# TensorE's order in a round of the two graph convolutions: eight sums together, the other work behind them

## The reference

```
xn  = layernorm(x)
# conv: twice, with its own weights
msg = relu(x[src]);  agg = segment_sum(msg, dst)
h   = relu((x + agg) @ w1 + b1) @ w2 + b2
# beside it a linear attention over all nodes
k, v = layernorm of (xn @ wk.T), (xn @ wv.T) per head;  kv = k.T @ v / S
x = x + relu(2 * conv(relu(conv(xn)))) + (xn @ wq.T) @ kv @ wo.T + bo
x = x + layernorm(x) @ weight.T + bias
```

## Time and profile before

| | us |
|---|---|
| median of 3 runs | 5125.66 |
| lowest and highest | 5112.02, 5127.13 |
| profiled execution | 5140.41 |
| its span in the trace | 5138.7 |
| first and last addition of the two convolutions | 225.1, 2500.5 |

### The profile page before, as it was taken

How to read it: one execution, slowest core, us unless ns; L and a number is a source line. 1 busy time by engine, 2 the same in 40 slices (tenths; PEclk the granted TensorE clock), 3 DMA queues, 4 the chain that set the end, 5 groups by cost and what they waited for, 6 DMA issues and landing times. The chain is left out here.

```text
span 5138.7 us, 69292 instructions
## 1 busy us (share of the span) xinstructions
PE 3250.9 (63%) x14347; PEld 2386.3 (46%) x14348; DVE 2963.7 (58%) x7108; ACT 1986.1 (39%) x4909; POOL 2901.0 (56%) x2929
## 2 busy tenths in 40 slices
PE   4477777777566677676677426666666532099980
PEld 1255555555455555555567414444444432066650
DVE  5677777777556666666556755555555584022223
ACT  0444444444333344343332135555555443033331
POOL 0377777777577777777204247777777735500006
PEclk6588888888778888888889758888888855599995
DMA  2434343433233333333212101111111342511115
GB/s 82 141 111 115 114 115 112 115 110 110 81 102 99 101 103 102 100 103 101 69 38 53 26 16 27 27 27 27 27 27 27 25 134 76 193 53 55 55 55 145
DMA packets 265996, 410.73 MB, mean 80 GB/s; under 512 B 77510, under 2 KB 182883, under 8 KB 265508
## 3 DMA queue, kind: packets, MB, share of 16 engines
q0 software_dynamic: 120320, 275.83, 21.3%
q1 hardware_dynamic: 145444, 132.39, 8.1%
HBM read 324.85 MB, written 83.11 MB: 79 GB/s over the span
## 5 line engine op out<-in xcount | busy, mean ns | idle before, releaser
L1463 PE MATMUL conv_ps<-conv_msg,conv_S 128*128 128x256 f32 x3328 | 1104.0, 481 | 596.7 <-DVE ACC L1473 265.7
L1463 PEld LDWEIGHTS conv_ps<-conv_msg,conv_S 128*128 128x128 f32 x3328 | 746.8, 238 | 836.4 <-issue 465.1
L1439 POOL DMA_INDIRECT conv_msg<-conv_table,GI x832 | 882.8, 1061 | 307.6 <-issue 259.2
L1439 POOL DMA_INDIRECT conv_msg<-relu_xn_table,GI x832 | 807.1, 970 | 358.4 <-issue 248.1
L1473 DVE TENSOR_TENSOR ACC<-ACC,conv_ps 128x256 f32 x1664 | 701.8, 422 | 515.2 <-issue 260.6
L2377 POOL DMA_INDIRECT gat_msg<-attn_table,GI x832 | 829.4, 997 | 266.6 <-issue 253.3
L2430 PE MATMUL gat_ps<-gat_M,gat_S 128*128 128x260 f32 x1664 | 596.1, 506 | 383.7 <-DVE ACC L2484 233.7
L1448 ACT ACTIVATE conv_S<-iota_row,LOC 128x128 f32<-128x128 f32 x1664 | 507.2, 387 | 387.8 <-PE conv_ps L1463 378.5
L2430 PEld LDWEIGHTS gat_ps<-gat_M,gat_S 128*128 128x128 f32 x1664 | 374.9, 245 | 528.2 <-issue 473.1
L3033 POOL DMA_INDIRECT combine_y<-expert_out,combine_at x98 | 94.5, 964 | 579.8 <-ACTq L3021 560.3
L2484 DVE TENSOR_TENSOR ACC<-ACC,gat_ps 128x260 f32 x832 | 350.2, 421 | 57.6 <-PE gat_ps L2430 23.1
(11 more groups left out here) (535 smaller groups left out, 5466.7 us busy)
## 6 DMA issues: line engine op xcount, KB each, us to landing
expert_in<-heads_zrow SPq DMA_DIRECT2D x53, 256.0 KB, 3.0
experts_xe<-expert_in SPq DMA_DIRECT2D x106, 128.0 KB
expert_out<-experts_y SPq DMA_DIRECT2D x106, 128.0 KB, 1.7
conv_msg<-relu_xn_table,GI POOLq DMA_INDIRECT x832, 2.8
conv_msg<-conv_table,GI POOLq DMA_INDIRECT x832, 2.8
gat_msg<-attn_table,GI POOLq DMA_INDIRECT x832
relu_xn_table<-begin_rx SPq DMA_DIRECT2D x49, 128.0 KB, 1.7
xnT<-begin_xt SPq DMA_DIRECT2D x49, 128.0 KB, 1.8
```

The source lines that it names most:

```text
L1439: pool.indirect_dma_start(self.msg[:, h * RING + k, :], None, table, bass.IndirectOffsetOnAxis(ap=self.m.GI[:, t:t + 1], axis=0)).then_inc ...
L1463: self.nc.tensor.matmul(self.ps[k % self.NB][:, 0:D], self.S[:, r % 2, k, :], self.msg[:, r % self.DEEP * RING + k, :], start=True, stop=T ...
```

## The change

In both convolution stages TensorE issues the eight sums of a round one after the other, and then the other work of the round. Before, four sums came, then the other work, and then four sums. The small matmuls at the end of an odd round stay last.

```
@@ stage_conv1, block.tensor
                 if r < ROUNDS:
                     rounds.pe_ready(pe, r)
-                    rounds.pe_sums(pe, r, 0, RING // 2)
+                    rounds.pe_sums(pe, r, 0, RING)
                 if here(i := turn_of(r, 4)):
                     kv.pe_sums(pe, i)
...
                 if here(u := turn_of(r, NodeNet.START + 1)):
                     net.pe_first(pe, u)
-                if r < ROUNDS:
-                    rounds.pe_sums(pe, r, RING // 2, RING)
                 if here(g := turn_of(r, 1, GROUPS)):
```

## The result

The changed kernel takes 5282.46 us (median of 4 runs, 5280.60 to 5286.83) against 5126.40 beside it: 1.0312 times the time before, with a 95% interval of 1.0292 to 1.0332. The forecast was slower, 5208 us, with a range of 5125 to 5305. Direction and range hold; the size was off by a factor of nearly two: +82 forecast, +156 measured.

The account below looks back on a forecast made before the run. VectorE's loop with ScalarE was taken to bound the first convolution, GpSimd's gathers the second. Over 48 pairs, 29 us and 53 us made 82 us on 5125.66, giving 5208 us, range 5125 to 5305.

Parts of the forecast that it names:

- What bounds each stage: First convolution: VectorE's pace, new waits paid in full; second: GpSimd's gathers, with 2.3 us a pair of slack for VectorE.
- Nothing is gained in the middle of the round: Side work between the sums was hidden behind VectorE's work; removing it gives at best GpSimd's 9.6 us in 400 us.
- rival C: Both convolutions: sums end earlier and GpSimd's waits for sums in the first go, 5100 us; chance 0.07.
- Second convolution, even round: Addition 3 to the odd round's addition 0 takes 6.5 us, 1.1 us above the slack: 53 us in all.
- First convolution, even round: Addition 3 to next sum 0 takes 5.7 to 7.4 us against VectorE's 6.14 us of work: 0.4 us a pair.
- another wait, which I have not priced, stands ahead of the first addition: Listed sign that the forecast is wrong: an unpriced wait ahead of a round's first addition; no size given.
- the likeliest case alone: Whole kernel: the narrower span of 5165 to 5260 us, inside the full range.
- First convolution, odd rounds: ScalarE's ReLU behind late side work delays finished rows only when one pair in eight starts low: 0.2 us a pair.
- The clock decides: Moved side work was expected to start at the lower clock in most pairs, losing 1.7 us or more.
- Rival A: Both convolutions: side work runs at the full clock and nothing changes, 5126 us; chance 0.14.
- Rival B: Both convolutions: low clock lasts through most even and part of odd side work, 216 us more, 5340 us; chance 0.15.
- The rule on keeping TensorE busy: TensorE in both convolutions: read naively, sums and side work run together at full clock, so the extra would be 0.

Follow-up runs that it names:

- root_first: The changed kernel, with ScalarE's square root put ahead of its copy of turned rows in the first convolution: 5218.26 us, 1.0190 times the kernel before.
- filler: The changed kernel, with matmuls nobody reads added on TensorE ahead of its waits for sums 4 and 6 of even rounds: 5146.65 us, 1.0056 times before.

## Why the prediction was right in direction and short in size

- **What bounds each stage**: right, as far as the runs show. The first convolution paid each new wait of VectorE in full; the second lost only what went beyond its slack, and there the gathers stopped being the bound.
- **Nothing is gained in the middle of the round**: right; no run showed a gain from it, and rival C (faster) is out.
- **Second convolution, even round**: 6.5 us from addition 3 to addition 0 and 53 us in all were forecast; the pair shown has 7.04 us, the mean of the 44 pairs is 7.0, and the stage grew by 66 to 81. The low clock covered the side work more fully than the 3.4 us that the earlier trace rows suggested, since it had fallen ahead of sum 4 and lasted from there to the end of the side work.
- **First convolution, even round**: the step that failed. The forecast compared sum 0 with VectorE's need and got 0.4 us a pair. It took VectorE's 6.14 us of own work as cover, and didn't ask what that work itself waits for. Its first instruction L444 needs ScalarE's root, which is queued behind the copy that needs the moved transposes. That wait is 1.9 us a pair where there were 0.3. root_first, which frees the root alone, gives 76 of the stage's 88 us back: some 54 at the end of even rounds, and 22 at the end of odd ones, whose side work then ran at the full clock in all pairs. The 12 that remain stand at the end of even rounds and are the forecast's own term (0.4 x 48 = 19). The prediction had named the case among its signs of being wrong ("another wait, which I have not priced, stands ahead of the first addition"), but gave it no price. Its range was wide enough to take it in; the likeliest case alone (5165 to 5260) was not. That the range holds is in part luck.
- **First convolution, odd rounds**: the ReLU's chain was named, and priced at 0.2 us a pair, 10 us, for one pair in eight with a low start. In the changed kernel 21 of 45 pairs had a low stretch in that side work and waited 2.09 us in place of 1.06: 0.5 us a pair, 22 us.
- **The clock decides**: right, and now shown. With the even rounds' side work at the full clock the changed order costs 29 us instead of 160 (filler), and 26 of these are the waits behind odd side work, nearly all in pairs where that still ran low. Rival A, whose rows were at the full clock, had the right price for that clock, but not the clock. Rival B had the size closer (216 us), but for the second stage 120 and for ScalarE's root nothing.
- **The rule on keeping TensorE busy** (the Trainium skill, TensorE: Matmul & The Clock Gate, "Why this matters for your kernels"): by it, idle gaps between bursts cost clock. The trace agrees: the clock fell within the 3.87 us idle, and was 0.50 from there through nearly all of the side work. It is the idea that eight sums in a row in the program are a burst on the engine that doesn't hold.

## What to carry to other kernels

When work is moved on one engine, follow each of its results to the engine that takes it, and list what stands behind the taker in that engine's own order: an unrelated step behind it may be on the path. Side work belongs where the consumer has long operations of its own ahead of its next need, or where the producer's clock is up. Don't price moved work at its profiled time: behind a stretch of short bursts that another engine paced, it ran here at the lower clock and took 1.91 us where the profile had 1.03 to 1.11.

## What the runs showed that I had not expected

Useless matmuls can pay: seven or eight of them per even round (five took 2.32 us in one pair of the second stage, at the full clock) took 131 us off the changed kernel. The granted clock was 0.94 in both stages instead of 0.82 and 0.79. And a square root of 0.21 us on ScalarE, which had been done in time, came to decide 76 us of the first stage through a change on TensorE that adds no work at all.
